# Scores from two fp32r parts in 64-row tiles, with maxima and exponential tiles side by side

## What is computed

```python
x1 = layer_norm(x); q = x1 @ q_w + q_b; k = ctx @ k_w + k_b; v = ctx @ v_w + v_b   # 16 heads of 16
scores = einsum('bhqd,bhkd->bhqk', q, k) * scale            # 256 x 512 per head
scores = where(mask, scores, finfo.min); attn = softmax(scores)
out = attn @ v; h = out @ cproj_w + cproj_b + x
h = h + gelu(layer_norm(h) @ fc_w + fc_b) @ proj_w + proj_b
out = h + alpha * (softmax((h @ w_q.T) @ (ctx @ w_k.T).T / 16) @ (ctx @ w_v.T) @ w_o.T)
```

## Time and profile before

| | us |
|---|---|
| median of 3 runs (lowest, highest) | 314.64 (312.69, 316.79) |
| span of the profiled execution | 310.4 (its own time is not shown apart) |
| TensorE busy | 268.6 |
| VectorE busy | 206.8 |
| ScalarE busy | 187.8 |
| GpSimd busy | 118.3 |

### The profile page before, as it was taken

One profiled execution on the slowest core, in us unless ns is written; L12 is line 12 of the kernel. 1 busy time (PEld: TensorE's weight loads), 2 busy tenths in 40 slices (PEclk: granted clock), 3 DMA queues, 4 the chain that ended last, 5 costly groups with the idle time before them and its releaser, 6 DMA issues.

```text
span 310.4 us, 5591 instructions
## 1 busy us (share of the span) xinstructions
PE 268.6 (87%) x2073; PEld 195.3 (63%) x2073; DVE 206.8 (67%) x367; ACT 187.8 (61%) x351; POOL 118.3 (38%) x174
## 2 busy tenths in 40 slices
PE   3974769998788999899979997999998989898995
PEld 2670236683266676665866766665966777677974
DVE  5774777729657859576569598657388655366854
ACT  1553367759464686967454887766466678426622
POOL 3574652523111369830012688430131256324100
PEclk9997599989797999999999999999999999999999
DMA  5597552522254002124112112121130000000001
GB/s 176 173 155 104 141 157 94 163 72 67 78 154 126 12 25 67 57 74 126 64 38 99 28 59 70 34 80 51 34 130 3 0 1 2 2 0 0 2 34 36
DMA packets 21163, 21.62 MB, mean 70 GB/s; under 512 B 4608, under 2 KB 17616, under 8 KB 21136
## 3 DMA queue, kind: packets, MB, share of 16 engines
q1 hardware_dynamic: 16880, 13.09, 14.8%
q0 software_dynamic: 1648, 3.87, 4.9%
q10 hardware_dynamic: 2608, 4.30, 4.6%
HBM read 10.50 MB, written 1.05 MB: 37 GB/s over the span
## 4 chain that ended last, share of the span: by engine, by line
PE 56%; ACT 13%; POOL 11%; DVE 9%; issue 5%; DMA 3%; ACTq 2%; POOLq 0%; DVEq 0%
PE work_ps L602 10%; PE om L679 8%; PE s L652 7%; PE work_ps L589 6%; PE s L669 6%; PE work_ps L606 5%; DVE neg_max L1442 4%; ACT q_stack L1100 3%; ACT probs L1109 2%; POOL y_l L1833 2%; PE s L602 2%; DMA q_stack<-qp 2%; POOL kf L1793 1%; ACT fx L1136 1%; POOL ft L1828 1%
## 5 line engine op out<-in xcount | busy, mean ns | idle before, releaser
L1442 DVE TENSOR_REDUCE neg_max<-s 128x1 f32<-128x512 f32 x128 | 83.5, 683 | 23.1 <-PE s L652 21.9
L1109 ACT ACTIVATE probs<-s 128x512 f32<-128x512 f32 x128 | 75.3, 601 | 32.4 <-PE s L669 31.8
L652 PE MATMUL s<-k_stack,q_stack 97*128 97x512 bf16 x128 | 49.8, 424 | 8.2 <-DMA q_stack<-qp 4.9
L669 PE MATMUL s<-q_stack,k_stack 109*128 109x256 bf16 x256 | 51.8, 286 | 2.0 <-ACT probs L1109 1.0
L679 PE MATMUL om<-probs,vals 128*17 128x256 f32 x512 | 34.5, 390 | 0.2 <-ACT probs L1109 0.2
L669 PEld LDWEIGHTS s<-q_stack,k_stack 109*128 109x128 bf16 x256 | 21.0, 102 | 19.0 <-ACT probs L1109 5.0
L652 PEld LDWEIGHTS s<-k_stack,q_stack 97*128 97x128 bf16 x128 | 13.0, 102 | 28.8 <-DVE neg_max L1442 14.3
L1763 POOL CAST max_cols<-neg_max 128x8 bf16<-128x8 f32 x16 | 6.1, 381 | 63.2 <-DVE neg_max L1442 63.2
L1100 ACT ACTIVATE q_stack<-om 13x1024 bf16<-13x1024 bf16 x16 | 16.3, 1017 | 9.1 <-PE om L659 8.8
L679 PEld LDWEIGHTS om<-probs,vals 128*17 128x17 f32 x512 | 12.0, 98 | 13.7 <-issue 6.2
L1123 ACT ACTIVATE y_h<-work_ps 128x512 fp32r<-128x512 f32 x12 | 7.2, 596 | 16.3 <-PE work_ps L606 14.5
(11 more groups left out here) (328 smaller groups left out, 724.5 us busy)
## 6 DMA issues: line engine op xcount, KB each, us to landing
k_stack<-kp SPq DMA_DIRECT2D x96, 64.0 KB
q_stack<-qp SPq DMA_DIRECT2D x81, 32.0 KB
cx<-in_ctx_dram SPq DMA_DIRECT2D x4, 512.0 KB, 4.7
pcx<-in_ctx_dram ACTq DMA_DIRECT2D x3, 512.0 KB, 3.6
xz<-in_x_dram SPq DMA_DIRECT2D x4, 256.0 KB, 2.7
raw_late<-in_L_xattn_fc_w_dram POOLq DMA_DIRECT2D x1, 1024.0 KB, 5.4
raw_late<-in_L_xattn_proj_w_dram POOLq DMA_DIRECT2D x1, 1024.0 KB, 6.7
h<-in_x_dram ACTq DMA_DIRECT2D x3, 256.0 KB, 2.6
```

The lines of the kernel that those rows point to most:

```text
L652: pe.matmul(s1[:, s1_bank(b, SLOTS * g + s), :], q_stack[0:ROW_MAX, hd, chunk(t)], k_stack[0:ROW_MAX, hd, :], start=True, stop=True).then_ ...
L669: mm = pe.matmul(s2[:, s2_bank(b, SLOTS * g + s), i * LQ:(i + 1) * LQ], k_stack[:, hd, chunk(k)], q_stack[:, hd, :], start=True, stop=True)
L1109: act.activation(probs[:, g % 2, s // 2, k:k + 2, :], s2[:, s2_bank(b, SLOTS * g + s), :].rearrange("p (k n) -> p k n", k=2), ACT.Exp).the ...
L1442: dve.tensor_reduce(neg_max[:, g % 2, s % 2, s // 2:s // 2 + 1], s1[:, s1_bank(b, SLOTS * g + s), :], AX.X, ALU.max, negate=True).then_inc ...
```

## The change

Queries and keys are split in two fp32r parts instead of three bf16 parts, three terms of 16 rows. With 8 rows for the maxima (two parts of 4 heads) and the mask row a stack has 57 rows, in one half of the array: even groups in rows 0 to 56, odd groups in rows 64 to 120. Matmuls over at most 64 rows from row 0 or 64 are issued as 64-row tiles of the array. The maxima tile of the next group thus lies in the other half than the exponential tile, and TensorE now issues it behind the slot's other step, directly ahead of the exponential tile (a second maxima tile of the slot behind it). The middle parts of queries and keys and two of the four steps of `split_max` are gone. The low part of the queries is now made by VectorE from the bank itself. One-hot rows of the keys for the maxima are built once by VectorE and copied by three DMAs at the start; rows 0 to 8 of the queries' stack (zeros, and the one of the mask) come by one more DMA per group (`stack_first`), so a group has 9 DMAs where it had 13.

```diff
-TERMS_Q = (0, 0, 1, 0, 1, 2)
-TERMS_K = (0, 1, 0, 2, 1, 0)
+TERMS_Q = (0, 0, 1)
+TERMS_K = (0, 1, 0)
+HALF = P // 2
+ROW_MASK = 2 * GH
+ROW_TERM = ROW_MASK + 1
+ROWS = ROW_TERM + len(TERMS_Q) * HD
...
-        with nc.sbuf_tensor("q_stack", [ROWS, H, LQ], BF16) as q_stack, nc.sbuf_tensor("k_stack", [ROWS, H, LK], BF16) as k_stack:
+        with nc.sbuf_tensor("q_stack", [P, H // 2, LQ], F32R) as q_stack, nc.sbuf_tensor("k_stack", [P, H // 2, LK], F32R) as k_stack:
...
+        def stack_rows(g, first, n):
+            return slice(g % 2 * HALF + first, g % 2 * HALF + first + n)
...   (SP, first instructions)
+                sp.wait_ge(dve_const, 4)
+                for g in range(NG):
+                    stack_first(g)
+                for g in range(1, NG):
+                    sp.dma_start(words(k_stack[stack_rows(g, 0, ROW_MASK), slots_of(g), :]),
+                                 words(k_stack[stack_rows(0, 0, ROW_MASK), slots_of(0), :])).then_inc(sel_in, 16)
                 sp.wait_ge(pre_full, U_CT + DC)
...   (TensorE)
-                pe.matmul(s1[...], q_stack[0:ROW_MAX, hd, chunk(t)], k_stack[0:ROW_MAX, hd, :],
+                half = stack_rows(g, 0, ROWS)
+                pe.matmul(s1[...], q_stack[half, hd, chunk(t)], k_stack[half, hd, :],
...
+            def attend(b, g, s):
+                nb, ng = ahead(b, g)
+                pb_, pg = behind(b, g)
+                tiles = MAX_TILES[s] if nb < B else ()
+                for i in tiles[:1]:
+                    max_tile(nb, ng, i)
+                if s == 0:
+                    pe.wait_ge(rows_in, NG * b + g + 1)
+                exp_tile(b, g, s)
+                for i in tiles[1:]:
+                    max_tile(nb, ng, i)
...
                 for at, ab, g, s, attends in slots(b, last):
-                    if attends:
-                        attend(ab, g, s, 0)
                     if not last and at in pre_at(b + 1):
...
                     if attends:
-                        attend(ab, g, s, 1)
+                        attend(ab, g, s)
...   (VectorE, queries)
+                elif n == U_Q:
+                    dve.wait_ge(qh_done, b + 1)
+                    for c in range(DC):
+                        i = dve.scalar_tensor_tensor(qp[1][:, c, :], pre_bank(b, n)[:, c * LQ:(c + 1) * LQ], bq[:, c:c + 1],
+                                                     qp[0][:, c, :].bitcast(F32), ALU.add, ALU.subtract)
+                    i.then_inc(pre_free, 1)
...   (GpSimd, split_max)
                 pool.tensor_copy(part[0], neg).then_inc(max_step, 1)
-                pool.wait_ge(max_step, step + 1)
-                pool.tensor_tensor(max_rest[:], neg, part[0], ALU.subtract).then_inc(max_step, 1)
-                pool.wait_ge(max_step, step + 2)
-                pool.tensor_copy(part[1], max_rest[:]).then_inc(max_step, 1)
-                pool.wait_ge(max_step, step + 3)
-                pool.tensor_tensor(part[2], max_rest[:], part[1], ALU.subtract).then_inc(max_split, 1)
+                pool.wait_ge(max_step, NG * b + g + 1)
+                pool.tensor_tensor(part[1], neg, part[0].bitcast(F32), ALU.subtract).then_inc(max_split, 1)
```

More of the change, by code:

```diff
@@ L127 @@
 V_LN1W, V_LN1B, V_VB, V_LN2W, V_LN2B, V_FCB, VECS = 0, 2, 4, 6, 8, 10, 18
[L128 removed]
+STACK_DMAS = 2 * len(TERMS_Q) + 2
 LATE_QUERIES = 2, 3
@@ L177, in build @@
         cx = sb("cx", [P, TK, D])
+        with nc.sbuf_tensor("ft_third", [P, 2 * LQ], F32) as ft_third:
+            pass
         zT = pair("zT", [P, DC, LQ])
@@ L513, in stack_queries @@
             def stack_queries(b, g):
-                made = ((pre_free, pre_use(b, U_Q)), (qm_done, b + 1), (q_parts, b + 1))
-                for part, (sem_, n) in enumerate(made):
-                    sp.wait_ge(sem_, n)
+                for part, (made, n) in enumerate(((qh_done, b + 1), (pre_free, pre_use(b, U_Q)))):
+                    sp.wait_ge(made, n)
                     for i in [i for i, p in enumerate(TERMS_Q) if p == part]:
-                        sp.dma_start(q_stack[i * HD:(i + 1) * HD, group(g), :], qp[rows_of(g), part, g // 2, :]).then_inc(stacked[g], 16)
+                        sp.dma_start(words(q_stack[term_rows(g, i), slots_of(g), :]), words(qp[part][rows_of(g), g // 2, :])).then_inc(stacked[g], 16)
             def stack_keys(b, g):
@@ L651, in max_tile @@
                     pe.wait_ge(pre_free, PRE_USES)
-                pe.matmul(s1[:, s1_bank(b, SLOTS * g + s), :], q_stack[0:ROW_MAX, hd, chunk(t)], k_stack[0:ROW_MAX, hd, :],
+                half = stack_rows(g, 0, ROWS)
+                pe.matmul(s1[:, s1_bank(b, SLOTS * g + s), :], q_stack[half, hd, chunk(t)], k_stack[half, hd, :],
                           start=True, stop=True).then_inc(s1_full, 1)
@@ L668, in exp_tile @@
                     k = 2 * (s % 2) + i
-                    mm = pe.matmul(s2[:, s2_bank(b, SLOTS * g + s), i * LQ:(i + 1) * LQ], k_stack[:, hd, chunk(k)], q_stack[:, hd, :],
+                    mm = pe.matmul(s2[:, s2_bank(b, SLOTS * g + s), i * LQ:(i + 1) * LQ], k_stack[half, hd, chunk(k)], q_stack[half, hd, :],
                                    start=True, stop=True)
@@ L995, in prologue @@
                 pe.wait_ge(w_lo, 3)
-                pe.wait_ge(sel_in, 16)
                 for s in range(START):
[L998 to L1018, removed]
+                    attend(0, 0, s)
+            def attend(b, g, s):
[9 more added lines that the diff above has]
+                    max_tile(nb, ng, i)
+                if s in PV_AT and pb_ >= 0:
+                    for k in PV_AT[s]:
+                        pv(pb_, pg, k)
+                if s == ROWS_AT and nb < B:
+                    max_rows(nb, ng)
             def tail_slot(at):
@@ L1328, in prologue @@
                 pre(0, U_V + 1)
-                rows(0, 0)
+                max_rows(0, 0)
                 for s in range(START):
@@ L1756, in split_max @@
             def split_max(b, g):
-                step = 3 * (NG * b + g)
-                part = [max_cols[:, :, ROW_MAX + i:ROWS:3] for i in range(3)]
+                part = [max_cols[:, :, g % 2 * HALF + i:g % 2 * HALF + ROW_MASK:2] for i in range(2)]
                 neg = neg_max[:, g % 2, :, :]
```

206 lines of the change are left out of this document (79 added, 127 removed).

## The result

The changed kernel takes **339.22 us** (median of 4 runs, 338.67 to 341.67) against 314.41 (4 runs, 312.69 to 316.79): **ratio 1.080, 95% interval 1.074 to 1.087**. The forecast was 316 us in a range of 296 to 330, with slower at 0.35. It is slower, and the time lies outside the range. The span 337.4 belongs to 339.22. In the recorded runs of the kernel before, 1.7 to 2.9 us lie around a span and not the 4.2 that I had inferred, so the span 310.4 must be that of 312.69, its fastest run here. I compare spans with spans.

What follows compares the result with a forecast made beforehand. TensorE's work, with waits between, was taken to set the pace. TensorE +8.6, query and key splits -3.4, maxima split -2, late maxima +1.4 and start -3 sum to +1.6 us: 314.6 becomes 316 us, range 296 to 330.

Steps and rivals of the forecast that it cites:

- slower at 0.35: Whole kernel: chance of 0.35 given to a time over 320.9 us.
- the 4.2 that I had inferred: Time around the profile's span: 4.2 us, from the 310.4 us span and the 314.64 us median of the runs.
- the term of +1.4 us: VectorE: maxima tiles issued later, and low halves queued behind their reductions, add 1.4 us; ends 0 and +12.
- rival 2: Slots 5 and 6 of each group: late maxima delay the row transposes, 12 us in the kernel, 328 us; chance 0.21.
- the low halves, at five places: VectorE: low halves of products wait behind maxima reductions, 0.4 us lost at each of five a period.
- the total of the crossings: TensorE array-mode changes around score tiles: 143 at 0.20 us, +28.6, plus 3.1 for 31 exits from L679.
- the factor of 0.7: Share of TensorE's added work, +12.3 us, taken to reach the kernel's end: +8.6 us; bounds 56% and 91%.
- The pair: Maxima tile and exponential halves run at once in opposite array halves: 90 pairs at 0.215 us, 19.4 us less TensorE work.
- The relief: Fewer steps: -3.4 us for splits of queries and keys, -2 for the split of maxima, -3 for the start.
- The start: First maxima tile's wait for the q_stack DMA shrinks from 4.9 us by 3: -3 us, ends 0 and -5.
- the wait of the row transposes: TensorE's wait for GpSimd's last split step, 9.9 us: shrinks if the forecast holds, grows if maxima come late.
- The steady period: One steady batch period, about 66 us: becomes 68; 61 would mean the crossings were free.

Runs made afterwards that it cites:

- e1: Kernel before, with only the issue order changed: maxima tile behind the slot's other step, directly ahead of the exponential tile; 329.96 us, ratio 1.056.
- e3: Changed kernel with all maxima tiles of a slot back ahead of its other step; 327.46 us, ratio 1.045 to the kernel before.
- e9: Changed kernel with only the maxima tiles of slots 8 and 9 (four of 32 a period) ahead of the slot's other step; 330.30 us, ratio 1.049.
- e2: Kernel before in its own order, score matmuls only over rows 64 and up, making them 64-row tiles in one half; 344.23 us, ratio 1.094.
- e4: Changed kernel with groups 0 and 1 in the lower half, 2 and 3 in the upper, so 45 of 90 pairs cannot overlap; 347.51 us, ratio 1.112.
- e7: Kernel before with two bf16 parts of queries, keys and maxima, third parts left out; rows, tiles, order and 13 DMAs stay; 307.69 us, ratio 0.976.
- e6: Changed kernel with maxima tiles ahead of the slot's other step in group 1 (slots 8 to 13) alone; 329.56 us, ratio 1.044.

## Why the prediction was wrong, step by step

**The step that failed** is the term of +1.4 us "for later maxima and for low halves queued behind them on VectorE". It measured 13 to 17 us (e1), 11 to undo (e3), 9 to 10 of them in four tiles a period (e9). I had given the mechanism a price of 12 as rival 2, which is near, but by luck: it was worked out for another place, slots 5 and 6, where a late maximum delays the split, and there the changed kernel waits less than before. The chain that decides is in slots 8 and 9: two maxima tiles behind transposes, two reductions, then a low half that frees the bank of TensorE's next transposes. I had named the low halves, at five places, and priced each at 0.4 us; in the trace one costs 1.6.

**The second term that failed** is the total of the crossings. Unit price and number held: 0.09 of drain each way and 0.10 of exposed 4-byte load. The total did not: for e2's edit my method gave 17 us, and it measured 27 to 30. I had counted at full clock throughout, and 13.3 us of e2's extra time lie in the first period, at 0.68 of it. In slots 16 to 31 of a steady period the crossings weigh even less than the factor of 0.7.

**The pair** held: it gives 0.22 us, and with the factor of 0.7 the 90 pairs bring 14 us, as forecast. In e4, 45 pairs less cost 8 to 10, where 7 were expected.

**What held besides.** The relief (8.4 against 8 to 9 in e7). The start, -1.9 against -3, and in part: the wait of the row transposes fell from 9.9 to 7.5. A group has 8 stack DMAs in all and not the 9 that the description and the prediction give: one of first rows, three of queries, four of keys. The steady period should have been 68; it is 72.3, and 68.8 with the maxima early.

**The sum again**, by span: 27.0 us = -1.9 start, +6.4 in the first period, +6.4, +8.5 and +7.6 in the others. Of these, e9 takes away 10.4 by four tiles a period. A bound for the clock: (1 - 0.919) x 337.4 - (1 - 0.960) x 310.4 = 27.3 - 12.4 = 15 us of full clock were granted less. Not all of it is lost time, since a waiting TensorE loses nothing by it, and it overlaps with the waits. In slots 7 to 15, where the changed kernel loses 6.8 us a period, three runs divide them: 1.5 are left with the maxima early and the clock at 1.00 (e3), 2.4 more come with the clock at 0.83 (e6), 2.9 more with the late tiles (the changed kernel, at 0.78).

**Open.** The clock by itself was isolated in that one stretch only. What makes it fall there is not shown: e6 comes to it behind 1.90 us of idle time and falls, e3 behind 1.77 and does not, the kernel before has 1.76 and keeps 1.00, and e2, with 1.77, falls. The fall is seen in kernels with 64-row tiles and not, in this stretch of the third batch, in before and e1. Nor is it shown why e2's first period fell to 0.68 with less waiting than the changed kernel's.

## What to carry to other kernels

Before an instruction is moved behind another, write out for every slot what the *consumer's* queue holds behind it, and who needs that: what I priced at 0.4 us a place became 9 to 10 us where two moved tiles, two reductions and a bank release stood in a row. Count half-array tiles by blocks: here a way in and a way out cost 0.19 us each with 4-byte weights, 0.38 a block, and a pair in it gives back 0.22, so by these prices a block needs two pairs to pay (an estimate; no run had longer blocks throughout). When a change has separable parts, price the plain one by itself: here the fewer parts won 8 us, and what was built around them cost some 32.

## What the runs showed of the hardware

- TensorE's granted clock can be at half for several us in which the engine is never idle: in e2 from 181.8 to 188.3, and over slots 7 to 15 it is busy 19.98 of 19.98 us at 0.83. The last idle time, 1.77 us, ended at 179.95. The kernel before has one of 1.76 us at the same place and keeps 1.00.
- What a low clock costs: the same sequence of matmuls took 5.25 us at 1.00 in e3 and 7.64 at 0.55 in e6. A wait need not bring the clock down: in the window shown, e1 waits 2.4 us in slots 7 to 15 and keeps 1.00.
- The clock goes with the spread of the runs: four runs of e7 have spans of 304.3, 305.1, 306.3 and 308.6 us at mean clocks of 0.978, 0.966, 0.961 and 0.956.
- A 64-row tile beside two others in the other half of the array costs nothing: 0.43 us with it and without it, 0.66 where it lies in the same half (e4).
- The 4-byte weights of a 64-row tile are not loaded ahead across the change of mode: the load starts with its tile, at 111.76, and the next half comes 0.22 us later. With bf16 weights it comes 0.12 later (e2).
